# Twelve wide copies instead of 48 narrow ones at the head of a causal attention block, an eight-bank ring and half-size transpose units

## The reference

```
x = L0(x)   # q,k of 32 channels, v of 256; softmax(q k) over all 1024 keys; gamma * out + x
x = L1(x)   # group norm, q,k,v of 256 channels, softmax(q k / 16), output product, + x
x = L2(x)   # layer norm; 8 query heads of 32, one key/value head; CAUSAL softmax; wo, + x,
            # layer norm, feed-forward (layer norm, w1, layer norm, gelu, w2), + residual
x = L3(x)   # as L1, with its own weights
```

## Time and profile before

| | |
|---|---|
| median of 3 runs | 1556.02 us (1555.89 to 1557.31) |
| profiled execution, its own time | 1558.38 us |
| its span, first to last instruction | 1556.6 us |
| PE busy | 1359.5 us (87%) |
| DVE busy | 871.3 us (56%) |
| ACT busy | 589.2 us (38%) |
| mean granted clock of TensorE | 0.928 of full speed |

### The profile page before, as it was taken

One profiled execution on the slowest core, in us unless ns is written; L12 is line 12 of the kernel. 1 busy time (PEld: TensorE's weight loads), 2 busy tenths in 40 slices (PEclk: granted clock), 3 DMA queues, 4 the chain that ended last, 5 costly groups with the idle time before them and its releaser, 6 DMA issues.

```text
span 1556.6 us, 22518 instructions
## 1 busy us (share of the span) xinstructions
PE 1359.5 (87%) x9152; PEld 1084.6 (70%) x9152; DVE 871.3 (56%) x1854; ACT 589.2 (38%) x877; POOL 92.3 (6%) x134
## 2 busy tenths in 40 slices
PE   6889948999998779999999849998899779899698
PEld 5778736777777657777777737776677656666586
DVE  3534436777456546766546625865655537774542
ACT  3423323353444314244435404342544323445232
POOL 0000000100000000100000000000001000011000
PEclk9889968999999869999999969999999969999799
DMA  5000010000000110000000010000000010000000
GB/s 168 1 0 1 28 42 15 17 12 1 1 1 1 38 31 22 25 25 1 1 1 1 1 41 11 22 25 15 1 1 1 14 28 25 18 14 3 14 1 27
DMA packets 27526, 27.10 MB, mean 17 GB/s; under 512 B 7329, under 2 KB 24225, under 8 KB 27425
## 3 DMA queue, kind: packets, MB, share of 16 engines
q1 hardware_dynamic: 27424, 25.67, 5.6%
HBM read 8.61 MB, written 4.19 MB: 8 GB/s over the span
## 4 chain that ended last, share of the span: by engine, by line
PE 76%; SPq 8%; DVE 8%; ACT 5%; issue 2%; DMA 1%; POOL 0%; DVEq 0%; ACTq 0%
PE ring L657 25%; PE ring L708 22%; PE ring L948 8%; SPq L573 7%; PE ring L930 5%; PE ring L700 5%; PE ring L917 4%; PE ring L857 1%; DVE part_max L1533 1%; ACT probs L1006 1%; PE ring L892 1%; PE ring L736 1%; ACT cprobs L1174 1%; DVE shift_max L1249 1%; PE ring L919 1%
## 5 line engine op out<-in xcount | busy, mean ns | idle before, releaser
L708 PE MATMUL ring<-probsT,vt 128*128 128x256 f32 x1536 | 362.2, 388 | 14.2 <-ACT probsT L1017 13.7
L708 PEld LDWEIGHTS ring<-probsT,vt 128*128 128x128 f32 x1536 | 288.0, 193 | 64.9 <-ACT probsT L1017 17.6
L1174 ACT ACTIVATE cprobs<-ring 128x1024 f32<-128x1024 f32 (+1 forms) x160 | 150.4, 940 | 269.0 <-PE ring L930 268.3
L1006 ACT ACTIVATE probs<-ring,neg_max 128x1024 f32<-128x1024 f32 x96 | 107.0, 1115 | 203.7 <-DVE neg_max L1250 92.8
L917 PE MATMUL ring<-ks,qs 96*128 96x512 f32 (+3 forms) x384 | 139.6, 442 | 46.3 <-issue 23.8
L1533 DVE TENSOR_REDUCE part_max<-ring 128x2 f32<-128x1024 f32 (+2 forms) x112 | 127.4, 1141 | 48.8 <-PE ring L919 28.7
L930 PE MATMUL ring<-qs,ks 98*128 98x256 f32 (+1 forms) x640 | 115.9, 305 | 43.3 <-DMA qs<-max_rows 37.1
L930 PEld LDWEIGHTS ring<-qs,ks 98*128 98x128 f32 x640 | 93.5, 197 | 65.4 <-DMA qs<-max_rows 38.5
L917 PEld LDWEIGHTS ring<-ks,qs 96*128 96x128 f32 x384 | 82.2, 224 | 64.2 <-issue 47.6
L1249 DVE TENSOR_REDUCE shift_max<-ring 128x1 f32<-128x1024 f32 x64 | 78.3, 1223 | 64.5 <-PE ring L657 61.8
L700 PE MATMUL ring<-consts,probs 128*128 128x128 f32 x768 | 103.4, 280 | 11.3 <-ACT probs L1006 4.2
(11 more groups left out here) (215 smaller groups left out, 2237.7 us busy)
## 6 DMA issues: line engine op xcount, KB each, us to landing
qs<-q_hi SPq DMA_DIRECT2D x256, 32.0 KB, 1.8
x<-x_dram SPq DMA_DIRECT2D x4, 1024.0 KB, 6.1
qs<-q_lo SPq DMA_DIRECT2D x128, 32.0 KB, 1.8
out_dram<-z SPq DMA_DIRECT2D x6, 512.0 KB, 2.8
qs<-max_rows SPq DMA_DIRECT2D x128, 2.0 KB
out_dram<-x SPq DMA_DIRECT2D x2, 512.0 KB, 2.8
raw_L_wv<-L_wv_dram SPq DMA_DIRECT2D x2, 256.0 KB, 5.9
raw_L_woT<-L_woT_dram SPq DMA_DIRECT2D x2, 256.0 KB, 6.2
```

The costliest lines, as they stand in the source:

```text
L708: last = mm(o[:, ct * QUARTER:(ct + 1) * QUARTER], vt[:, j, ct * P:(ct + 1) * P], probsT[:, qi % (NQ - 1), j, :], start=j == 0, stop=j == ...
L1006: A(probs[:, ti % 2, :], flat(full_name(l, b, ("s", ti))), ACT.Exp, bias=neg_max[:, ti:ti + 1], accum_out=row_sum[:, ti:ti + 1]).then_inc( ...
L1174: A(causal_probs(step, n), heads(name)[:, :, 0:n], ACT.Exp).then_inc(read_done["c", "act"], 1)
```

## The change

Four things change together.

1. `stacks` is called three times for an image instead of eight: for queries 0 to 511 of both head groups (12 copies of 32 x 2 x 512 floats), and later for each of the quarters 2 and 3 (12 copies of 32 x 2 x 256 floats). `qs` keeps its size, with another layout. The number of these copies goes from 96 to 36 for an image, their bytes stay.
2. `fills` makes the maxima and the shift of block k + 1 (from k = 3 on) in the first two thirds of block k, instead of those of block k + 2 over all of block k. The copies for quarter 2 are issued behind shift 3, those for quarter 3 behind shift 5.
3. `acc` is a unit of the ring like the others, which now has eight banks; it is opened at the first values of a block.
4. A transposed tile is two units of one bank with four transposes each, and ACT copies each with an instruction of its own.

The strings in ORDER are new throughout. A part of the diff (of the strings one line):

```diff
-RING = 7
+RING = 8
     "PE": (
-        "0F2eF02F4Fg02F40Fg24F02FFF3F50F24FFF5F02e6FFF0c3FFF64F024F0F2404F20F42F06FFF4F20F46FFF2F04c6FFF06FFFec0F4F0c"
+        "0F2eF60F2Fe50F72d5F401F756FFF3F750F62d7FFF0F6572d4FFF017FFF05F204F6F2046F012F405F710FFF2F456F012FFF3Ff70120F"
...
     elif k == 1:
-        ahead = [("q2", 1)] + ahead[:2] + [("kv", 1)] + ahead[2:] + [("vt", 1)]
-    out = evenly(ahead, 0, places) if ahead else []
+        ahead = [("q2", 1)] + max_events(3) + [("shift", 3), ("kv", 1)]
+    elif k == 2:
+        ahead = [("vt", 1)]
+    else:
+        ahead = max_events(k + 1) + [("shift", k + 1)] if k + 1 < K else []
+    out = evenly(ahead, 0, places if k < 3 else 2 * places // 3) if ahead else []
...
-        qs = shared("qs", [P, STACKS, 4, QUARTER], r_s, F32R)
+        qs = shared("qs", [P, HG, 4, 2 * QUARTER], r_s, F32R)
...
-            def stacks(b, k):
+            def stacks(b, q0, n):
+                wait_read(sp, f"C{b}.q2{q0 // 2}")
+                if q0:
+                    wait_filled(sp, causal_name(b, last_exp[HG * (q0 - 1) - 1]))
+                elif b:
+                    wait_filled(sp, causal_name(b - 1, last_exp[K - 1]))
+                at = (q0 % 2) * QUARTER
+                for a in range(4):
+                    for g, src in enumerate((q2[0], q2[0], q2[1])):
+                        sp.dma_start(qs[DH * g:DH * (g + 1), :, a, at:at + n].bitcast(F32),
+                                     src[DH * a:DH * (a + 1), :, q0 * QUARTER:q0 * QUARTER + n].bitcast(F32)
+                                     ).then_inc(stack_in[q0 // 2 + q0 % 2], 16)
...
                 for b in range(B):
-                    for k in range(STACKS):
-                        yield from stacks(b, k)
-                    yield from shifts(b, 0)
-                    yield from shifts(b, 1)
-                    for k in range(2, K):
+                    yield from stacks(b, 0, HALF)
+                    for k in range(K):
                         yield from shifts(b, k)
-                        if k + 2 >= STACKS and k + 2 < K:
-                            yield from stacks(b, k + 2)
+                        if k == 3 or k == 5:
+                            yield from stacks(b, k // 2 + 1, QUARTER)
...
-                for j in range(NT):
-                    last = nc.tensor.transpose(o[:, j, :], probs[:, ti % 2, j * P:(j + 1) * P], ident)
+                for j in range(TPH):
+                    last = nc.tensor.transpose(o[:, j, :], probs[:, ti % 2, (TPH * hf + j) * P:(TPH * hf + j + 1) * P],
+                                               ident)
...
                 if jt == 0:
-                    if b or k:
-                        wait_read(pe, f"C{b}.o{k - 1}" if k else f"C{b - 1}.o{K - 1}")
+                    open_unit(name)
                     wait_read(pe, f"C{b}.vt{BLOCKS[k][1] // 2}")
+                acc = slot(name)[:, 0, :]
```

More of the change, by code:

```diff
@@ L50 @@
[L50 to L54, removed]
@@ L219, in causal_units @@
                 if is_final(e):
-                    out.append((causal_name(b, e), "act", 0))
+                    out.append((causal_name(b, e), "act", 1))
             elif e[0] not in NO_UNIT:
@@ L228, in queries, with causal_openings @@
     return QUARTER - max(jt * P - BLOCKS[k][1] * QUARTER, 0)
+def causal_openings():
+    width = {u[0]: u[2] for u in causal_units()}
+    out = [u for u in width if u[0] == "p"]
+    for b in range(B):
+        for e in causal_schedule():
+            if e[0] not in NO_UNIT and (e[0] != "values" or e[2] == 0):
+                out.append(causal_name(b, e))
+    return [(name, width[name]) for name in out]
 def ring_places(order):
-    full, causal = ([u for u in units if u[2]] for units in (full_units(), causal_units()))
-    queues = {"0123456": iter(full), "abcdefg": iter(causal)}
+    queues = {FULL_BANKS: iter([(u[0], u[2]) for u in full_units()]), CAUSAL_BANKS: iter(causal_openings())}
     place, previous = {}, {}
@@ L240, in ring_places @@
                 at = banks.index(ch)
-                name, _, width = next(units)
+                name, width = next(units)
                 place[name] = at
@@ L251, in weave @@
     for ch in order:
-        next(full if ch in "F0123456" else causal)
+        next(full if ch in "F" + FULL_BANKS else causal)
     assert next(full, None) is None and next(causal, None) is None
@@ L431, in build @@
         y_out = sem("y_out")
-        stack_in = [sem(f"stack_in{i}") for i in range(STACKS)]
+        stack_in = [sem(f"stack_in{i}") for i in range(3)]
         shift_in = [sem(f"shift_in{i}") for i in range(2)]
@@ L902, in stage, with stack @@
                 yield
+            def stack(k, a, rows, lo, hi):
+                hg, qi = BLOCKS[k]
+                at = (qi % 2) * QUARTER
+                return qs[0:rows, hg, a, at + lo:at + hi]
             def causal_max(b, e):
@@ L916, in causal_max @@
                     a = i if two == 2 else 2 * two + i
-                    last = mm(o, qs[0:3 * DH, k % STACKS, a, at:at + P], ks[0:3 * DH, lo:hi], start=True, stop=not diag)
+                    last = mm(o, stack(k, a, 3 * DH, at, at + P), ks[0:3 * DH, lo:hi], start=True, stop=not diag)
                     if diag:
@@ L930, in causal_exponents @@
                     last = mm(heads(name)[:, a, 0:n], ks[0:3 * DH + 2, jt * P:(jt + 1) * P],
-                              qs[0:3 * DH + 2, k % STACKS, a, QUARTER - n:QUARTER], start=True, stop=True)
+                              stack(k, a, 3 * DH + 2, QUARTER - n, QUARTER), start=True, stop=True)
                 last.then_inc(filled["c"], 1)
@@ L1014, in turned @@
             def turned(l, b, ti):
-                name = full_name(l, b, ("t", ti))
-                wait_filled(act, name)
-                nc.scalar.copy(probsT[:, ti // 2 % (NQ - 1), :, (ti % 2) * P:(ti % 2 + 1) * P],
-                               slot(name).rearrange("p b (s n) -> p (b s) n", n=P)).then_inc(read_done["f", "act"], 1)
+                for i in range(2 * ti, 2 * ti + 2):
+                    name = full_name(l, b, ("t", i))
+                    js = slice(TPH * (i % 2), TPH * (i % 2 + 1))
+                    wait_filled(act, name)
+                    nc.scalar.copy(probsT[:, ti // 2 % (NQ - 1), js, (ti % 2) * P:(ti % 2 + 1) * P],
+                                   slot(name)[:, 0, :].rearrange("p (s n) -> p s n", n=P)
+                                   ).then_inc(read_done["f", "act"], 1)
+                    yield
             def values(l, b, i):
```

107 lines of the change are left out of this document (55 added, 52 removed).

## The result

The changed kernel takes 1484.94 us (median of 4 runs, 1483.02 to 1486.26); the kernel before took 1555.95 us beside it (4 runs). The ratio is 0.9542, 95% interval 0.9525 to 0.9559: 4.6% faster. The forecast was 1483 us.

A forecast was written before the change was run, and what follows sets the result against it. The prediction took SP's issue of stack copies, which stops PE at the image heads and lowers its clock, as the bound. 1558.4 - 58 - 26 + 8 + 3 = 1485.4, with runs 2.4 us under the profiled one: 1483 us, range 1448 to 1532.

The forecast's parts named there:

- The bound and its cause: Heads of the four images: PE's stops follow issues in SP's queue, not transfers; 72.1 us of 197 us idle.
- Price of a wide copy: SP's queue: a 32 x 2 x 512 copy costs 0.63 us with the gap, so 12 take 7.6 us.
- Idle time at the heads, -58 us: PE's waits at first exponents and "max" scores: of 72.1 us, 8.5 and 5.6 stay, 58 us go.
- Two signs: Image heads: first `max_rows` copy some 15 us after the first stack copy; clock in the four heads 0.85 or above.
- The clock, -26 us: PE at the heads: of 42 us lost to the lowered clock, 26 come back; bounds 10 and 42.
- Shorter lead, +8 us: The 16 shifts of blocks 4 to 7, now one block ahead: some stops of PE, +8 us, bounds 0 and +32.
- Half units, +3 us: ACT's 192 half-size copies to `probsT`: 17 us more ACT work, +3 us of time, bounds -7 and +17.
- The accumulator, 0: PE's removed wait at L948 for ACT's copy of the sums: worth 0, bounds -10 and +10.
- Covers are taken from elsewhere: Rival: work now covering the heads is missing elsewhere, half the idle and clock gain lost; 1525 us, chance 0.20.
- Costly wide copies: Rival: a wide copy costs SP in proportion to its rows, 1.2 us each; 1519 us, chance 0.07.
- Late shifts: Rival: PE stops at first exponents of blocks 4 to 7; at 6 us each 1571 us, slower, chance 0.05.
- Copies hidden by the transfer: Rival: issue is small beside transfer, so fewer, wider copies end no sooner; time stays at 1556 us, chance 0.02.

The follow-up runs named there:

- late12: Changed kernel with twelve tiny copies on SP's queue ahead of the shift copies of blocks 4 to 7; 1540.69 us, ratio to before 0.9891.
- wide_before: Kernel before with only the 48 narrow copies at an image's head made 12 wide ones, orders kept; 1501.88 us, ratio to before 0.9643.
- split_head: Changed kernel with only the wide copies at an image's head each in two (24 issues); 1521.30 us, ratio to before 0.9786.
- narrow_after: Changed kernel with narrow copies again, a semaphore for each block, new order, ring and units kept; 1544.82 us, ratio to before 0.9921.
- split_after: Changed kernel with every wide copy in two, 24 issues at a head and for each later quarter; 1551.80 us, ratio to before 0.9961.
- split_later: Changed kernel with only the copies for quarters 2 and 3 in two (24 issues each); 1518.29 us, ratio to before 0.9763.

## Why the prediction was right, step by step

*The bound and its cause.* Right. That SP's issue time, not the transfers, held PE at the heads is shown from both sides: twelve wide copies at each head of the old kernel take 55 us off, narrow ones in the new kernel (48 at a head) put 60 back, 24 at each head 36.

*Price of a wide copy.* Taken as 0.63 us with the gap; twelve take 7.8 us. The rows of 2 and of 32 partitions were the right neighbours.

*Idle time at the heads, -58 us.* It went from 72.1 to 5.5 us (with the 2.6 us at L750), 67 less, since the order covered more than my count gave it: at the first "max" 4.1 us are left and not 8.5, at the exponents 1.4 and not 5.6. Two signs did not come as written. I expected the first shift copy some 15 us after the first stack copy, and it came after 21.4, because PE's order puts the shift there. It cost nothing, as PE has work for this time. And the clock in the head of image 0 is 0.84, just under the 0.85 that I had named.

*The clock, -26 us.* PE's busy time fell by 21.5 us; the terms as written (12.6 + 11.2 - 3, and a quarter of 18.2) make 25.4. The direction and the cause are right, but that the size came near is in part luck. By the measure that I used, busy time times the missing clock, the heads went from 42 to 14.5 us (43.31 x 0.16 + 44.09 x 0.10 + 45.52 x 0.07), the 27.6 us less that the term wants. But over the whole run the same measure goes from 98 us (1359.5 x 0.072) to 56 (1338.0 x 0.042), 42 less, where busy time fell by half of that. It overstates what the clock costs in this comparison, and I had no row that tied it to busy time.

*Shorter lead, +8 us.* No wait of its kind is in the trace (the one for `max_rows` that is left, at 525.22 us, is the head of image 1), and four copies more in the way bring 0.7 us. The count of PE's work between shift and exponents, less the 4.5 us of the path, is nearly borne out by late12: ten places of the eleven. What came of the term is the other thing that I had named, a shift too close behind its last reduction. PE waits for `max_cols` ahead of a shift for 8.0 us in four places, where it was 1.4 in one. Two of them are shifts of blocks 4 to 7, as many as I had counted:

```profile
295.46 0.38 PE L902 MATMUL ring<-consts,max_cols 128*8 128x128 f32 x2 [1.46 <-DVE max_cols L1576]
...
1339.72 0.59 PE L902 MATMUL ring<-consts,max_cols 128*8 128x128 f32 x2 [3.02 <-DVE max_cols L1576]
```

These are shift 5 of image 0 and shift 7 of image 3, 4.5 us where the term had 8. The other two (0.88 and 2.68 us) are shift 2 of images 0 and 2, which the term did not cover. Besides, against the kernel before, PE waits 5.2 us more at L760, 3.1 more at L723 for `probs`, 2.5 more for `an`. What in the new order or the ring brings these was not tried.

*Half units, +3 us.* The size of ACT's extra work was wrong (I had added up the durations of single copies): 6.1 us (595.3 against 589.2), not 17. The group of the half copies in the changed kernel, by form, in the columns of the earlier trace rows:

```profile
L1049 ACT COPY probsT<-ring 128x512 f32<-128x512 f32 x192 | 102.3, 592 | 48.2 <-PE ring L723 48.2
```

192 x 592 ns would be 113.7 us, but the busy time is 102.3: the second copy of a pair starts some 0.12 us (11.4 / 96) before the first one's record ends, so durations of neighbours do not add. The timeline shows it too: a pair from 80.15 us on takes 1.07 us in all. The waits for `probsT` grew from 13.7 to 16.4 us, and the 3 us fit.

*The accumulator, 0.* Right for the wait, by the run that puts it back; the bank itself was not tested alone.

*The sum.* The terms that were off cancel: 67 instead of 58 us at the heads, against 16 us of new waits elsewhere instead of 11, and 21.5 us of clock instead of 26. That the total is nearer than its parts is luck.

*The rivals.* "Covers are taken from elsewhere" holds in small: idle time fell by 50.9 us in all, 67 at the heads, so 16 us came back elsewhere; the rival had set 29. The comparison of wide_before and the changed kernel says the same: 20 us fewer of waits at the first "max", yet only 5.2 us less of idle time (151.4 to 146.2), and 12.0 us less of busy time, which is where the last 17 us come from. "Costly wide copies" was priced at 1519 us, and split_head, which costs just that at the heads, took 1521. "Late shifts" was to decide from a path of 11 to 13 us on; twelve tiny copies make one of 12.3 (4.5 + 7.8), and the kernel was at 1540.69 us still faster than before, by 1.1%, so the point at which it turns lies farther out than I had put it: ten of the sixteen places stopped, for 3.4 us each by the mean, where the rival had all sixteen stop for 5. (The 78 us that the rival had to eat up should read 81, 58 + 26 - 3, which is still 5 us for each place.) "Copies hidden by the transfer" is excluded by the three runs with other counts of copies and the same bytes. But the prediction's words there, "the issue is the longer part", hold for the queue and not for one copy: a narrow copy takes 590 ns to issue and 1.8 us to land. The landings overlap each other and the issues do not, so of a stack's 9.0 us 7.6 are issue.

## What to carry to other kernels

A queue of small copies is work in series: when the engine that matters waits for one semaphore, count the issues ahead of it in the queue, times the issue time of one, before looking at bytes. Where an order is fixed, the margin of a hand-over can be read off it beforehand (work between producer and consumer, less the length of the path), and such a count told ten of eleven places here with 7.8 us more in the way, but two of five with 2.5 us. Price a stop of PE with the clock that follows it. Where one wait hands over the work of two blocks, a wait for each lets the first one go after half of the issues.

## What the runs showed of the hardware

The issue time of a copy into `qs` on SP's queue hardly depends on its size: by the medians 563 ns for 2 KB, 590 for 32 KB, 597 for the wide ones of 64 and 128 KB. The 1024 KB loads of x take less, 376 ns. The wide copies take 2.0 us (64 KB) and 2.3 us (128 KB) to land, the narrow ones 1.8.

A stop of PE costs more than its length. Against the changed kernel, idle and busy time of PE rose by 24.4 and 10.2 us in split_head (span 1518.8, busy 1348.2), by 36.9 and 21.1 in narrow_after, by 36.4 and 19.3 in late12, by 41.0 and 18.8 in split_after, and by 16.8 and 19.0 in split_later. For each microsecond that PE stood still, its matmuls took 0.4 to 1.1 us more, with the granted clock at 0.938 to 0.945 over the run instead of 0.958. What decides within this range is not shown: the four stops of 2.3 to 4.8 us in split_later cost the most for their length, but the ten of 0.5 to 5.7 us in late12, as far apart, half of that. Two windows of split_later with one such stop each, and a third without one:

```profile
250.00:300.00 50.00, 45.30 (x346) 34.68 (x338) 35.16 (x71) 18.07 (x28) 4.95 (x7) 0.93 0.05 13
300.00:350.00 50.00, 42.92 (x290) 33.40 (x291) 33.39 (x74) 18.42 (x33) 3.57 (x5) 0.90 0.06 17
...
400.00:450.00 50.00, 50.00 (x402) 39.44 (x401) 21.90 (x50) 19.00 (x28) 3.47 (x5) 1.00 0.01 2
```

The first two windows in the changed kernel, which has neither stop:

```profile
250.00:300.00 50.00, 46.81 (x399) 36.47 (x402) 39.77 (x88) 20.80 (x34) 4.96 (x7) 1.00 0.04 10
300.00:350.00 50.00, 47.07 (x341) 36.13 (x341) 40.43 (x83) 22.88 (x40) 3.57 (x5) 1.00 0.07 17
```
